# A graph network on one core: the low part of a split chunk without the second rounded copy in PSUM

## The reference, cut to what matters

```python
def layer0(x, src, dst):                      # N = 6250, D = 512, H = 1024
    agg = segment_sum(x[src], dst, N)         # gather 100000 rows, add by destination
    h = (1.0 + eps) * x + agg
    h = relu(batch_norm(h @ W1 + b1))         # 512 -> 1024
    h = relu(batch_norm(h @ W2 + b2))         # 1024 -> 512
    return x + h
x = layernorm(x + layer0(x, src, dst))

def layer1(x, src, dst):
    agg = segment_sum(x[src], dst, N)
    h = where(indegree > 0, agg, x)
    return batch_norm(relu(h @ W.T + b))      # 512 -> 512
x = layernorm(x + layer1(x, src, dst))
```

## Time and profile before

| | us |
|---|---|
| median of three runs | 2925.01 |
| lowest, highest | 2919.75, 2929.12 |
| profiled execution, own time | 2951.29 |
| its span on the core | 2949.5 |
| TensorE busy | 2402.7 (81%) |
| VectorE busy | 1447.7 (49%) |
| ScalarE busy | 1022.3 (35%) |
| GpSimd busy | 1555.5 (53%) |

### The profile page before, as it was taken

One profiled execution on the slowest core, in us unless ns is written; L12 is line 12 of the kernel. 1 busy time (PEld: TensorE's weight loads), 2 busy tenths in 40 slices (PEclk: granted clock), 3 DMA queues, 4 the chain that ended last, 5 costly groups with the idle time before them and its releaser, 6 DMA issues. The chain is left out here.

```text
span 2949.5 us, 42174 instructions
## 1 busy us (share of the span) xinstructions
PE 2402.7 (81%) x9711; PEld 1593.3 (54%) x9712; DVE 1447.7 (49%) x2269; ACT 1022.3 (35%) x1776; POOL 1555.5 (53%) x1731
## 2 busy tenths in 40 slices
PE   4888888887888887889997487978898787878885
PEld 2555555555555555578886354544444454445454
DVE  4444444444444444453336555545554454555448
ACT  2444444444444444455555311111111111111126
POOL 6565656666566666300002466666666666666633
PEclk9989989999999999999997698988898898988886
DMA  7666666666666676433326666665666666666668
GB/s 244 191 207 199 201 191 203 193 208 203 192 205 201 195 205 203 136 105 98 97 83 175 232 190 186 185 192 167 190 185 186 185 187 190 181 194 180 185 179 270
DMA packets 164329, 545.46 MB, mean 185 GB/s; under 512 B 30979, under 2 KB 34906, under 8 KB 159522
## 3 DMA queue, kind: packets, MB, share of 16 engines
q0 software_dynamic: 125120, 410.09, 48.3%
q1 hardware_dynamic: 17608, 78.33, 8.7%
q10 hardware_dynamic: 21544, 56.48, 5.6%
HBM read 493.18 MB, written 51.60 MB: 185 GB/s over the span
## 5 line engine op out<-in xcount | busy, mean ns | idle before, releaser
L848 PE MATMUL psum<-ring,select 128*125 x2400 | 1272.5, 632 | 71.7 <-issue 66.2
L595 POOL DMA_INDIRECT ring<-x_in,src_t x782 | 740.6, 947 | 479.1 <-issue 213.2
L595 POOL DMA_INDIRECT ring<-x_d,src_t x782 | 755.8, 967 | 430.0 <-issue 215.8
L962 ACT ACTIVATE rows_hi<-ring 128x512 fp32r x606 | 376.4, 630 | 851.4 <-issue 505.9
L884 PE MATMUL psum<-sumsT_hi,w_hi 128*128 128x250 f32 x1248 | 580.7, 465 | 97.6 <-DVE sumsT_lo L721 65.9
L848 PEld LDWEIGHTS psum<-ring,select 128*125 128x125 f32 x2400 | 433.6, 200 | 271.9 <-issue 238.6
L698 DVE TENSOR_TENSOR rows_lo<-ring,psum 128x512 fp32r<-128x512 f32 x404 | 277.5, 687 | 599.8 <-issue 323.8
L833 PE MATMUL psum<-rows_hi,select_r 128*125 128x512 f32 x600 | 372.2, 620 | 65.0 <-DVE rows_lo L698 36.3
L884 PEld LDWEIGHTS psum<-sumsT_hi,w_hi 128*128 128x128 f32 x1248 | 248.8, 199 | 277.8 <-issue 201.5
L884 PE MATMUL psum<-sumsT_lo,w_hi 128*128 128x250 f32 x1248 | 360.8, 289 | 40.2 <-issue 38.7
L884 PE MATMUL psum<-sumsT_hi,w_lo 128*128 128x250 f32 x1248 | 361.8, 290 | 37.5 <-issue 37.5
(11 more groups left out here) (191 smaller groups left out, 2495.2 us busy)
## 6 DMA issues: line engine op xcount, KB each, us to landing
hidden_d<-of_layer ACTq DMA_DIRECT2D x25, 1000.0 KB
act_f<-hidden_d SPq DMA_DIRECT2D x24, 1000.0 KB
ring<-x_in,src_t POOLq DMA_INDIRECT x782
ring<-x_d,src_t POOLq DMA_INDIRECT x782
sums<-x_in ACTq DMA_DIRECT2D x50, 224.0 KB
sums<-x_d ACTq DMA_DIRECT2D x50, 224.0 KB
rows_r<-x_in SPq DMA_DIRECT2D x6, 1120.0 KB
x_d<-rows_r SPq DMA_DIRECT2D x6, 1120.0 KB
```

Of the source, the lines that this page charges most:

```text
L595: nc.gpsimd.indirect_dma_start(slot(c % S), None, table, bass.IndirectOffsetOnAxis(ap=index_of(c), axis=0)).then_inc(gathered[c % S], 16)
L848: whole = nc.tensor.matmul(agg(h), select[h][:, WHOLE_AT.index(p), :], of_chunk(pe, first, place), start=False, stop=n + 1 == WINDOW, skip ...
L962: high = nc.scalar.activation(rows_hi[:, k, :], of_chunk(act, first, SPLIT_AT[k]), ACT.Copy)
```

## The change: what it does

`high_ps` and its activation go. ScalarE rounds a split chunk once, into `rows_hi`; the wait for `split_lo` of the row before goes with the bank, and so does `AHEAD`. VectorE subtracts `rows_hi[:, k, :]` from the chunk in both layers. Layer 1's instructions stay as they were.

```diff
-        high_ps = m.bank(5)
-        AHEAD = 1 if layer == 0 else 0
...
-                if layer == 0:
-                    nc.vector.sem_inc(split_lo, AHEAD)
...
                         dve.wait_ge(split_hi, SPLIT * (2 * v + h) + k + 1)
-                        high = high_ps if layer == 0 else rows_hi[:, k, :].bitcast(F32)
-                        nc.vector.tensor_tensor(rows_lo[:, k, :], of_chunk(dve, first, SPLIT_AT[k]), high, ALU.subtract
-                                                ).then_inc(split_lo, 1)
+                        nc.vector.tensor_tensor(rows_lo[:, k, :], of_chunk(dve, first, SPLIT_AT[k]),
+                                                rows_hi[:, k, :].bitcast(F32), ALU.subtract).then_inc(split_lo, 1)
...
-                            pe.wait_ge(split_lo, SPLIT * tile_use + k + 1 + AHEAD)
+                            pe.wait_ge(split_lo, SPLIT * tile_use + k + 1)
...
                         act.wait_ge(split_used, SPLIT * (2 * v + h) + k + 1)
-                        if layer == 0:
-
-                            act.wait_ge(split_lo, SPLIT * (2 * v + h) + k + 1)
                         act.wait_ge(landed, begin + (SPLIT_AT[k] + 1))
                         high = nc.scalar.activation(rows_hi[:, k, :], of_chunk(act, first, SPLIT_AT[k]), ACT.Copy)
-                        if layer == 0:
-                            high = nc.scalar.activation(high_ps.bitcast(F32R), of_chunk(act, first, SPLIT_AT[k]),
-                                                        ACT.Copy)
                         high.then_inc(split_hi, 1)
```

## The result

The change made the kernel faster by 0.6% where 4.5% were forecast: 2907.44 us median (2905.73 to 2909.66, five runs) beside 2929.12 (2919.75 to 2931.26, five runs) for the kernel before, ratio 0.994, 95% interval 0.9923 to 0.9956. The profiled execution has a span of 2905.7 us.

A forecast was written before the change was run, and what follows sets the result against it. Bound: a chain of latencies in layer 0's gather, with TensorE waiting for late VectorE. Terms -34 - 70 - 8 - 30 + 10 = -132 took 2951.3 to 2819 us profiled, 2794 median; range 2740 to 2895, own range 2740 to 2845.

The forecast's parts named there:

- row chain: Layer 0 split rows: a ScalarE-VectorE round trip through one PSUM bank, 2.30 us a row, 36.8 of a 48.7 us pair.
- Row wait: TensorE's wait at L833, first matmul of a split chunk: 39.8 us, forecast -34 with rows ready up to eight ahead.
- Sums wait: TensorE's wait at L817, the clear inside the turn, for both tiles' sums: 82.6 us, forecast -70.
- Low part: Low part of the sums, 10.2 us of L884's idle time, made behind rows 4 and 5: forecast -8.
- The rest of L884's idle time: TensorE's idle time at L884 apart from the low part's 10.2 us; claimed to stay.
- Clock: TensorE's granted clock in the gather was to rise from 0.93 to 0.96 with less standing: forecast -30 us.
- Port: VectorE's second SBUF operand lengthens layer 0 gathers: 38 us of GpSimd time, 10 us put on the path.
- GpSimd: Claimed not to bound layer 0: its 260.8 us of pauses are waits for free slots, the ring being as good as full.
- Rival D: No difference: time returns as TensorE waits elsewhere, or GpSimd's pauses leave just the port's cost as gain; 2925 us, chance 0.08.
- C: Rival: GpSimd paces layer 0 by its own pauses, so longer gathers add 38 us; 2963 us median, chance 0.07.
- B: Rival: only the row wait goes, the sums stay late; 2878 us median, chance 0.20.
- P: Rival: the shared port blocks GpSimd for each whole subtraction, 11.0 us a pair; 2955 us median, chance 0.03.

The follow-up runs named there:

- e5: Kernel after with layer 0's 16 product pieces at places 20 to 35 instead of 14 to 36; ratio 0.9934 to the kernel before.
- e7: Kernel after with the turn at place 12 instead of 7 and the product pieces at places 20 to 34; ratio 0.9996 to the kernel before.
- h1: Kernel after with every second gather of layer 0 left out from the 35th on; 2667.91 us, ratio 0.8976 to the kernel before.
- h2: Kernel before with every second gather of layer 0 left out; 2817.11 us, ratio 0.9478 to the kernel before.
- e1: Kernel before with the PSUM copy gone and VectorE reading the SBUF row, but the wait for `split_lo` left; ratio 0.9967 to the kernel before.
- p1: Kernel after with half of layer 0's gathers each replaced by a GpSimd TENSOR_SCALAR over the slot; ratio 0.9015 to the kernel before.
- n1: Kernel after with layer 0's gathers from the 35th on fetching 512-byte rows instead of 2 KB; ratio 0.9945 to the kernel before.
- r17: Kernel after with layer 0's gathers for ring slots 17 to 33 left out, so 17 follow each other; ratio 0.9270 to the kernel before.

## Why the prediction was wrong

The prediction took the row chain for the only thing that held ScalarE's reads of TensorE's results. The late increments held them too, and they stayed.

**Row wait, right.** 39.8 to 14.5 us, -25 where -34 was forecast. ScalarE's roundings run free of the subtraction. In e5 and e7, though, 44.6 and 156.5 us came back in this very place.

**Sums wait, the step that failed.** The prediction had TensorE's last product end at 675.65, ScalarE "still in the row chain", and said that with the rows done earlier "the read starts near 675.9 and the sums are ready near 678.9". In that very place of the kernel before the increment of `product_done` is recorded at 685.16, 0.02 us ahead of the read at 685.18; the matmul that makes it is the last of the product:

```profile
675.36 0.29 PE L884 MATMUL psum<-sumsT_hi,w_lo 128*128 128x250 f32 x1
```

The read could not have started before. It is not the case everywhere: of the 25 last products of a pair before, 12 reads come over 1 us after the product's end and within 0.4 us of a recorded increment; in the others the row chain was the later of the two, or the increment was not recorded. Two reasons lay over each other: ScalarE was busy or waiting in the row chain while the increment was under way. In the kernel before only 3 of 100 product reads have ScalarE idle before the product ends; in the kernel after 94 of 104 do, and 56 of them start over 1 us after the product's end, 290 us in all. The wait at L812 fell by 49.5 us, but the low part (10.2 to 46.0) and the other products' waits (+9.7 and +9.2) gave it back. With hardly any late increments (h1, h2) this step holds: the wait ahead of the clear goes from 86.2 to 0.0 us. That the sum holds there too, 5.7 us a pair where 5.3 were forecast, is in part luck: the wait for split rows, priced at -34, does not shrink (9.6 to 11.8), and the rest comes with the clock, from 0.95 to 1.00, more than was forecast for it.

**Low part, -8, wrong in sign.** It was put at next to nothing left, as made behind two rows. It is made from the high part, the first work that waits for `turned` and `product_done`, both from TensorE, and so takes on their lateness: +36. The rest of L884's idle time, taken to stay, grew by another 25 us; that L884 grew by 61 us in all where 8 were to go is the largest gap in the sum, before the clock's 30 and the 20 short at the clear.

**Clock, wrong in sign.** 0.93 to 0.96 was forecast, 0.91 came. It was derived from standing that mostly did not go (211 to 185 us), and TensorE's busy time of 40.6 us a pair did not change, so nothing came of the 30 us. In h1, where TensorE never stands, it is 1.00.

**Port, right.** 996 against 945 ns, 51 ns for each of 755 gathers, 38.6 us; 38 was forecast. Spread over 404 subtractions that is 0.095 us each. e1 (998 ns with the wait kept) and h2 (945 ns with half of the gathers and the operand in PSUM) point to the operand. By the rule of the Trainium skill's page "SBUF — State Buffer", section "Who interferes with whom", taken at full strength as the prediction did, it would be up to the whole 0.687 us; the measurement is a seventh of it.

**GpSimd, half right.** "GpSimd waits for TensorE" and "the ring is as good as full" took its pauses for want of slots. I compared each pause, less the usual 0.3 us, with the end of the matmul that frees the slot. Of 91 pauses over 1 us of the kernel before (234 us), 69 (171 us) had the slot free before GpSimd's last gather ended; after, 61 of 79 (137 of 178 us). In these the slots were free, the word of it was late. The pauses sank from 260.8 to 201.2 us and the gathers took 39 of these 60 us.

Rival D had the number (no large difference, "waits elsewhere on TensorE ... mid-product"), and its second half, that the pauses leave just the gain that the port takes, comes nearest to what the rows show. C had the right place, GpSimd's pauses, but as its own. B and P did not come about: the sums wait fell by more than half, and the mean gather of the kernel after stays at 1.0 us (the highest of any run is 1.085, in p1; P wanted over 1.2).

## What to carry to other kernels

Before pricing a wait as removed, look at what else would have ended it: match the waiter's start with the record of the increment, not with the end of the instruction that makes it. Two waits on the same stretch hide each other, and taking away the upper one shows the lower one. In a kernel whose GpSimd issues indirect gathers back to back, count on signals from TensorE that come microseconds late (1.7 to 2.0 in the mean here). Moving the reader to a later place did not help here (e5, e7); fewer gathers did (p4, which leaves out about a quarter of them: 8.0% off the kernel before, against 0.6% for the change alone), and of the same number, alternating ones did better than 17 on end (0.898 against 0.927). With all gathers made, only asking for two slots at a time gave anything, about 0.3%, and that within the intervals.

## What the runs showed of the hardware

- While GpSimd issues indirect gathers at 1.25 us each, TensorE's semaphore increments are held up (late share 0.59 to 0.65 in layer 0, 0.61 to 0.68 in layer 1; 0 of 49 without gathers) and come out mostly once it has run dry, in the place shown in order and 0.04 us apart; mean lateness 1.7 to 2.0 us, single ones over 10. The increments of the other engines are not (0.00 to 0.02). It does not depend on the bytes (n1: 0.61 at a quarter of them) nor on GpSimd being busy (p1: 0.00); it depends on how many gathers there are and how closely they follow (p4 0.51, r17 0.27, h1 0.06). By what path is open (the issuing, the descriptors or the transfers' own increments, which n1 all left as they were), and so is whether the write to PSUM or only the increment is late.
- Some of ScalarE's register instructions take 0.70 us in place of 0.09, in episodes; one lies at 674 to 678 us in the kernel after, where the increment of `turned` is 11.9 us late (676.93 to 688.85). They go with the gathers too: 38 of 862 in the kernel after last over 0.55 us, 7 of 862 in h1 and 2 of 862 in p1. Whether the two go together otherwise is open.
- With VectorE's subtraction reading two operands in SBUF in place of one, gathers take 996 ns in place of 945 (e1 998, h2 945).
